# Second attention's scores: four matmuls of 32 stationary columns in place of one of 128, on the same 50 rows

## The reference, cut to what matters

```python
x = x + _L0_attn_ref(_layernorm(x), Mq, Mk, Mv)      # 8 heads, scores 1024x1024 per head, softmax
x = x + _L0_ffn_ref(_layernorm(x), gate, up, down)   # 704 wide, FP4 quantize and dequantize
x = x + _L1_attn_ref(_layernorm(x), ...)             # the one of the change
x = x + _L1_ffn_ref(_layernorm(x), ...)              # top 2 of 8 experts of rank 16

def _L1_attn_ref(x, w_qkv, b_qkv, ...):              # 16 heads of 16 features
    q = _ln(q, g_q, be_q) * HD ** (-0.5)
    k = _ln(k, g_k, be_k)
    attn = jax.nn.softmax(jnp.einsum('bhqd,bhkd->bhqk', q, k), axis=-1)
    out = jnp.einsum('bhqk,bhkd->bhqd', attn, v)
```

## Time and profile before

| what | value |
|---|---|
| median of 3 runs | 2958.23 us |
| span of the profiled execution (first to last instruction) | 2954.7 us |
| TensorE busy | 2580.8 us, 87% |
| VectorE busy | 2104.1 us, 71% |
| ScalarE busy | 1979.9 us, 67% |
| granted TensorE clock, mean | 0.969 |

### The profile page before, as it was taken

How to read it: one execution, slowest core, us unless ns; L and a number is a source line. 1 busy time by engine, 2 the same in 40 slices (tenths; PEclk the granted TensorE clock), 3 DMA queues, 4 the chain that set the end, 5 groups by cost and what they waited for, 6 DMA issues and landing times.

```text
span 2954.7 us, 115301 instructions
## 1 busy us (share of the span) xinstructions
PE 2580.8 (87%) x50178; PEld 1403.9 (48%) x50178; DVE 2104.1 (71%) x4266; ACT 1979.9 (67%) x3763; POOL 1193.4 (40%) x1677
## 2 busy tenths in 40 slices
PE   4766786998989989999889989899889999899697
PEld 3434554445644466444554456444654446444233
DVE  6778766866778488875879578775788667775433
ACT  3541255876668866787668866787668776687684
POOL 3563156215642167223653156322662256411210
PEclk9997999999999999999999999999999999999798
DMA  4212332234424252323424253243423253222310
GB/s 127 44 38 46 67 84 69 50 49 86 97 64 81 47 111 62 77 51 73 109 63 75 34 108 79 58 78 58 103 70 66 49 86 84 63 67 47 87 31 16
DMA packets 470460, 203.52 MB, mean 69 GB/s; under 512 B 283289, under 2 KB 459937, under 8 KB 469929
## 3 DMA queue, kind: packets, MB, share of 16 engines
q1 hardware_dynamic: 467960, 194.07, 31.9%
q10 hardware_dynamic: 1968, 1.72, 0.2%
HBM read 46.48 MB, written 32.51 MB: 27 GB/s over the span
## 4 chain that ended last, share of the span: by engine, by line
PE 42%; DVE 29%; ACT 8%; SPq 7%; issue 7%; DMA 5%; POOL 2%; DVEq 0%; ACTq 0%; POOLq 0%
PE pR L459 18%; PE pV L690 9%; DVE nmaxa L1239 8%; PE pS L459 5%; PE pS L650 5%; ACT ub L953 5%; PE pV L560 3%; SPq L1958 2%; PE pR L469 2%; SPq L2155 2%; SPq L2141 1%; DMA xT<-ua 1%; DMA xT<-xhb 1%; DVE ua L1142 1%; DVE ua L1119 1%
## 5 line engine op out<-in xcount | busy, mean ns | idle before, releaser
L953 ACT ACTIVATE ub<-pS 128x512 f32<-128x512 f32 x2048 | 1048.2, 612 | 227.6 <-PE pS L650 227.0
L1239 DVE TENSOR_REDUCE nmaxa<-pS 128x1 f32<-128x1024 f32 x512 | 621.1, 1214 | 249.9 <-PE pS L459 247.2
L914 ACT ACTIVATE ua<-pS,nmaxa 128x1024 f32<-128x1024 f32 x384 | 427.9, 1114 | 406.1 <-DVE nmaxa L1239 403.9
L459 PE MATMUL pS<-ua 128*32 128x512 f16 x8192 | 544.1, 387 | 102.2 <-ACT ua L914 77.4
L690 PE MATMUL pV<-ub,vaug 128*17 128x512 f32 x4096 | 536.7, 597 | 14.6 <-DVE ub L1397 13.2
L1726 POOL TENSOR_TENSOR ua<-ua,rz 128x256 f32<-128x256 f32 x512 | 332.0, 650 | 429.4 <-DVE rz L1256 414.4
L650 PE MATMUL pS<-ub 50*128 50x512 f16 x1920 | 352.0, 386 | 27.6 <-DMA ub<-scr 11.6
L459 PEld LDWEIGHTS pS<-ua 128*32 128x32 f16 x8192 | 210.1, 98 | 273.9 <-ACT ua L914 110.4
L459 PE MATMUL pR<-wgu,xT 128*32 128x352 f16 x6144 | 284.9, 321 | 49.5 <-DMA xT<-ua 24.6
L650 PEld LDWEIGHTS pS<-ub 50*128 50x128 f16 x1920 | 96.5, 93 | 404.4 <-ACT ub L953 334.6
L560 PE MATMUL pV<-ua 128*32 128x128 f32 x6144 | 244.7, 279 | 22.6 <-DVE oTa L1250 12.2
(11 more groups left out here) (262 smaller groups left out, 4062.6 us busy)
## 6 DMA issues: line engine op xcount, KB each, us to landing
ua<-ua SPq DMA_DIRECT2D x384, 128.0 KB, 2.7
ub<-scr SPq DMA_DIRECT2D x264, 64.0 KB, 2.9
scr<-ub SPq DMA_DIRECT2D x30, 512.0 KB, 3.8
x<-in_L_attn_x SPq DMA_DIRECT2D x8, 1024.0 KB, 6.2
between<-x SPq DMA_DIRECT2D x7, 1024.0 KB, 5.0
ub<-between SPq DMA_DIRECT2D x7, 1024.0 KB, 5.9
out<-ub SPq DMA_DIRECT2D x7, 1024.0 KB, 5.4
ub<-scr SPq DMA_DIRECT2D x192, 32.0 KB, 1.8
```

Source lines behind the costliest of these rows:

```text
L459: i = e.matmul(dst[j:j + 32], w[:, j:j + 32], m, start=start, stop=stop)
L914: e.activation(EA[n % 4], pS[:, 1024 * (n % 2):1024 * (n % 2) + 1024], ACT.Exp, bias=nmaxa[:, n % 32:n % 32 + 1], accum_out=zz[:, n % 8:n ...
L953: e.activation(EB[(4 * n + hl) % 8], pS[:, 512 * hl:512 * hl + 512], ACT.Exp).then_inc(e1_in, 1)
L1239: e.tensor_reduce(nmaxa[:, n % 32:n % 32 + 1], pS[:, 1024 * (n % 2):1024 * (n % 2) + 1024], AXX, ALU.max, negate=True).then_inc(max0_in, 1)
```

## The change

`attn1` on TensorE calls `by_columns` for the scores of a head. The stationary operand (keys, 50 rows by 128) is cut into four of 50x32; each is multiplied with the same 50x512 of the queries, and writes 32 of the 128 partitions of the head's bank. The signal to ScalarE stands on the fourth. Values, rows and banks are the same, nothing else differs.

```diff
@@ attn1, TensorE
                             row, o = head_at(hg, hl)
-                            e.matmul(pS[:, 512 * hl:512 * hl + 512], kk_[row:row + 50, o, 128 * c:128 * c + 128],
-                                     q[row:row + 50, o, 512 * qh:512 * qh + 512]).then_inc(s1_in, 1)
+                            by_columns(pS[:, 512 * hl:512 * hl + 512], kk_[row:row + 50, o, 128 * c:128 * c + 128],
+                                       q[row:row + 50, o, 512 * qh:512 * qh + 512], True, True).then_inc(s1_in, 1)
```

## The result

The kernel after took 2971.1 us, the median of 5 runs (2965.45 to 2977.47), beside 2960.36 us for the kernel before (5 runs, 2956.24 to 2965.4): ratio 1.0044, 95% interval 1.0025 to 1.0063. Repeated with more runs on another occasion it was 1.0033 (1.0020 to 1.0046), 9.8 us. So the change is slower by 6 to 14 us by the longer comparison (7 to 19 by the first), a little clear of no change.

What follows compares the result with a forecast made beforehand. TensorE was taken to bound 330 of 512 steps: 6.9 us there plus a tenth of 3.8 us elsewhere, about 7.5, made the span 2954.7 into 2962.2; with runs 3.5 us above the profile, 2966 us, range 2950 to 3010.

Steps and rivals of the forecast that it cites:

- The matmuls (1): Scores of a step: two sets of 8 matmuls replace two pairs; 21 ns more a step, bounds 7 and 45.
- The weight loads (2): Score loads on TensorE: 16 loads of 32 columns for 4 of 128, hidden behind streaming, costed at nothing.
- The change of shape (3): Into and out of a step's scores: shape still changes, 0.09 us each way, so 0.18 us per step is kept.
- My one row: Two transposes in the preparation: a change of rows with the same 128 columns costs 0.09 us more.
- The signal (4): Signal to ScalarE: a head is done 11 ns later with its fourth matmul, which lies inside the 21 ns.
- The sum: 330 late steps x 21 ns = 6.9 us, plus a tenth of the other 182 steps' 3.8 us; about 7.5 us.
- one of the two signs of a wrong forecast: Wrong if the gap into or out of the scores is not 0.09, or 330 is no good count of steps.
- 330 that count and 182 that hide nearly everything: Of 512 steps, TensorE comes late in 330 and is the bound; in 182 the 0.40 us bank wait covers additions.
- A: Scores cut in strips: row halves no longer overlap, 0.44 us more a step, time about 3140 us; chance 0.11.
- B: Scores: second set's loads wait for the first, 0.12 us a step, 40 to 61 us, 2998 to 3019; chance 0.08.
- C: Scores: columns alone decide the shape, so a step saves 0.16 us, time 2876 to 2905 us; chance 0.11.

Runs made afterwards that it cites:

- The two strips: Against the kernel before, each head's scores as two matmuls of 64 stationary columns; 1.0018 (1.0006 to 1.0031).
- the mixed kernel: Against the kernel before, heads 0 and 1 in four column strips each, heads 2 and 3 whole; 1.0104 (1.0076 to 1.0132), 31 us slower.
- four strips (again): The change itself measured once more beside the kernel before; 1.0033 (1.0020 to 1.0046).
- 128 rows, full: Against the kernel before, scores replaced by sixteen strips per step on 128 rows of constant operands, all 512 query columns; 1.0172 (1.0145 to 1.0198), 51 us more.
- one half: Against the kernel before, all four heads read from partitions 0 to 49, real scores of half the heads left out; 1.0414 (1.0394 to 1.0435), 123 us.
- 128 rows, half: Against the kernel before, scores replaced by sixteen strips per step on 128 rows of constant operands, 256 query columns; 0.9872 (0.9855 to 0.9889), 38 us less.

## Why the prediction was right

Forecast were 2966 us, 7.5 more than before, in a range of 2950 to 3010; measured were 2971.1, and 10 to 11 more than before.

*The matmuls (1).* Right. Foreseen were 21 ns between the last starts, measured 20; seven distances of 3.3 ns. The second set did not start earlier than before.

*The weight loads (2).* Right for the change: 89 ns and hidden. The two strips showed what this may rest on: at 64 columns the load takes 103 ns and the second set starts 14 ns later. The strips' shorter loads give back 3 ns on the way in, which I had not counted.

*The change of shape (3).* Right: 306 ns from the last start to the next group in both kernels. My one row, rows changing at 128 columns, carried over. The runs show each kind: rows at 32 columns (the two 128-row kernels no longer pay the 0.1 us each way), columns at 50 rows (the mixed kernel, 0.12 us).

*The signal (4).* Not measured by itself. ScalarE's idle time for the scores rose by 7.2 us in one trace of the change and by 12.7 in the other; less than 10 was foretold.

*The sum.* Its mechanism was right, the count of steps was not, one of the two signs of a wrong forecast that I had named. (Its terms also add up to 7.3 and not 7.5.) I had 330 that count and 182 that hide nearly everything. The periods of the steps, before and after, taken as the median over the first six sequences, grow by 13 to 19 ns in 51 of the 63; few hide it, and one shrinks by 100 ns. They sum to 0.74 us for a sequence (0.92 in the second trace), 6 to 7 us for eight. Carried over to all eight sequences that is about 410 of the 512 steps, each with 17 ns where I had 21: two errors that nearly cancel, so that the number came out as near as it did is partly luck.

A step paced by ScalarE hides a long delay and not a short one. The mixed kernel shows it: 45 of its 63 periods grow by 120 to 126 ns, and eight shrink by 101 to 103, which gives most of the delay back; under the change the same eight grow, by 6 to 13 ns. The times of the kernels with a known difference per step (the doses) go the same way, though not in order of size:

| kernel | more per step, us | time, us | steps' worth |
|---|---|---|---|
| four strips (again) | 0.017 | 9.8 (5.9 to 13.6) | 350 to 800 |
| mixed | 0.122 | 31 | 250 |
| 128 rows, full | 0.222 | 51 | 230 |
| one half | 0.428 | 123 | 290 |
| 128 rows, half | -0.205 | -38 | 185 |

(The third column is the ratio's share of the kernel before, the last one is it over the second.) So 330 is too high for the four large doses and too low for the small one. For the change this leaves 6 to 7 us shown in the steps; the measured 9.8 has an interval that reaches down to 5.9, and where the rest is, if it is there, stays open; stops for instructions are the candidate.

*The rivals.* A (no overlap of the halves in strips) is out: 0.63 and not 1.05 us. B (uncovered loads) is out for the change, with a gap of 226 and not 330 ns between the sets. C (columns alone decide) is out by the 306 ns and the two 128-row kernels.

## What to carry to other kernels

Cutting a matmul into column strips saves nothing by itself: streams of one shape already overlap where they touch different rows, and each further matmul of a set delays the last start by 3 ns. What is worth having is a common shape with the neighbours, rows and columns both, for which this kernel would gain 0.2 us a step; cutting the columns alone leaves that cost where it was. And a price per step is multiplied with the steps in which it is not hidden, whose number depends on how large the price is: here some 410 steps for 17 ns, and 185 to 290 for 0.12 us and more.

## What the runs showed of the hardware that I had not expected

- With 50 rows of fp16, a load of 64 columns takes 103 ns, one of 128 takes 93, one of 32 takes 89.
- Two matmuls on the same rows are listed 7 ns apart in a group that takes no longer than two overlapping pairs (0.54 us), while four on one half take 0.97: the starts of the trace don't tell which matmuls overlap.
- With 32 matmuls in a step, TensorE stopped 27 times for 34.6 us in all, waiting for nothing that the profile names, the 14 longest of them in or just after a 16 KB packet of the instruction queue, which at random would be the case for 6 in 10.
